# A Mamba-2 layer with a gated LoRA branch: B times C and the sum of squares as column halves right behind the mixing, and x's transposes ahead of the state's product

## What is computed

```
proj = xn @ in_proj_w.T                       # gate 4096, x 4096, B 1024, C 1024, dt 64
xBC  = silu(conv_bias + sum_k pad(hbc)[k:] * conv_weight[:, k])      # 4 taps
dt_p = softplus(dt + dt_bias);  dA = exp(dt_p * A)
state = state * dA_t + (dt_p * x)_t * B_t;    y_t = state . C_t      # for every token
y  = y + x * D
yn = y * rsqrt(mean(y * y over the 512 channels of a group) + EPS) * norm_weight * silu(gate)
out = yn @ out_proj_w.T
```

## Time and profile before

| | |
|---|---|
| three runs, us | 1832.69, 1836.27, 2473.83 |
| median, us | 1836.27 |
| profiled execution, us | 1833.52 |
| its span, first to last instruction, us | 1831.7 |
| mean granted TensorE clock | 0.994 |
| busy: TensorE, weight loads | 1791.5 (98%), 1425.5 (78%) |
| busy: VectorE, ScalarE, GpSimd | 1526.6 (83%), 812.5 (44%), 1170.5 (64%) |
| HBM | 119 GB/s over the span |

### The profile page before, as it was taken

The page is one execution under the profiler, slowest core; times in us unless marked ns, Lnnn a source line. Parts: engine busy times, 40 slices in busy tenths (PEclk is TensorE's granted clock), DMA queues, the critical chain, the costliest instruction groups (busy, mean ns, idle before and its releaser), DMA issues.

```text
span 1831.7 us, 29420 instructions
## 1 busy us (share of the span) xinstructions
PE 1791.5 (98%) x10904; PEld 1425.5 (78%) x10904; DVE 1526.6 (83%) x1945; ACT 812.5 (44%) x1803; POOL 1170.5 (64%) x1149
## 2 busy tenths in 40 slices
PE   6989999999999999999999999999999999999997
PEld 4777877878787787878777787777878778787875
DVE  6868888888888888888888888888888888888887
ACT  4554353444435344443544434354444435444442
POOL 5437557574755757475697847658574765857478
PEclk9999999999999999999999999999999999999998
DMA  7542224232333423333564333323232323323233
GB/s 244 162 132 104 104 104 138 84 125 104 104 105 103 138 89 120 104 105 108 181 228 140 125 104 123 104 102 129 76 128 102 122 104 104 132 75 117 91 126 130
DMA packets 113502, 220.70 MB, mean 120 GB/s; under 512 B 10448, under 2 KB 46672, under 8 KB 113360
## 3 DMA queue, kind: packets, MB, share of 16 engines
q1 hardware_dynamic: 112320, 218.66, 35.7%
q10 hardware_dynamic: 1040, 0.16, 0.1%
HBM read 204.63 MB, written 14.16 MB: 119 GB/s over the span
## 4 chain that ended last, share of the span: by engine, by line
PE 87%; DVE 4%; POOL 3%; ACT 2%; issue 2%; DMA 1%; SPq 0%; POOLq 0%; DVEq 0%; ACTq 0%
PE ps_conv L1148 9%; PE ps_conv L1151 9%; PE ps_conv L1154 7%; PE ps_y L1308 6%; PE ps_out L1151 6%; PE ps_out L1148 6%; PE ps_gate L1148 6%; PE ps_gate L1151 6%; PE ps_y L1313 5%; PE ps_s L1336 5%; PE ps_out L1154 5%; PE ps_gate L1154 4%; PE turned_x L1234 3%; PE ps_conv L1155 2%; PE ps_g L1273 2%
## 5 line engine op out<-in xcount | busy, mean ns | idle before, releaser
L801 DVE SCALAR_TENSOR_TENSOR xc<-ps_conv,convw_sb,xc 128x511 f32<-128x511 f32 (+2 forms) x576 | 429.8, 746 | 26.2 <-ACT xc L589 12.0
L1083 POOL TENSOR_TENSOR rstd_col<-mean_square,half 128x1 f32<-128x1 f32 x128 | 105.5, 825 | 541.2 <-ACT mean_square L719 541.2
L974 DVE TENSOR_TENSOR decay<-decay,ps_g 128x1024 f32<-128x1024 f32 x128 | 155.9, 1218 | 175.6 <-PE ps_g L1346 175.6
L910 DVE TENSOR_TENSOR_SCAN decay<-decay,eye 128x1024 f32<-128x1024 f32 x128 | 297.6, 2325 | 0.6 <-DMA decay<-decays_d 0.6
L595 ACT ACTIVATE xc<-xc 128x512 f32<-128x512 f32 x192 | 120.9, 631 | 381.6 <-DVE xc L801 380.8
L1101 POOL TENSOR_TENSOR cpre<-cpre,xc 128x1024 f32<-128x1024 f32 x112 | 267.5, 2388 | 0.0
L1148 PE MATMUL ps_conv<-xn_hi,wconv_hi 128*128 128x512 f32 x768 | 242.4, 437 | 0.0
L1151 PE MATMUL ps_conv<-xn_hi,wconv_lo 128*128 128x512 f32 x768 | 207.1, 392 | 0.0
L1308 PE MATMUL ps_y<-decay,dtx 128*64 128x128 f32 x2048 | 197.4, 279 | 2.1 <-DVE decay L974 1.9
L728 ACT ACTIVATE square<-ps_y 128x512 f32<-128x512 f32 x128 | 76.7, 599 | 244.0 <-DVE ps_y L925 244.0
L1148 PEld LDWEIGHTS ps_conv<-xn_hi,wconv_hi 128*128 128x128 f32 x768 | 140.1, 193 | 49.1 <-issue 29.9
(11 more groups left out here) (206 smaller groups left out, 3734.3 us busy)
## 6 DMA issues: line engine op xcount, KB each, us to landing
decay<-decays_d SPq DMA_DIRECT2D x128, 512.0 KB, 5.3
cpre<-rows_d SPq DMA_DIRECT2D x112, 512.0 KB, 3.9
stage<-w_in_t SPq DMA_DIRECT2D x32, 1024.0 KB, 6.5
stage<-w_out_t SPq DMA_DIRECT2D x16, 1024.0 KB, 5.3
stage<-w_in_t SPq DMA_DIRECT2D x32, 256.0 KB, 3.3
out_sum<-hidden SPq DMA_DIRECT2D x16, 256.0 KB, 6.1
ffn_d<-sgate SPq DMA_DIRECT2D x16, 256.0 KB, 2.4
out<-out_sum SPq DMA_DIRECT2D x16, 256.0 KB, 3.8
```

What stands on the lines that cost most here:

```text
L801: e.scalar_tensor_tensor(acc[:, d:], ps[:, 0:BLK - d], convw_sb[:, tile, TAPS - 1 - d:TAPS - d], acc[:, d:], ALU.mult, ALU.add).then_inc(S ...
L910: e.tensor_tensor_scan(d[:, :], d[:, :], eye8[:, :, :].rearrange("p h i -> p (h i)"), 0.0, ALU.mult, ALU.add).then_inc(S["scan"], 1)
L974: e.tensor_tensor(by_head(d[:, :]), by_head(d[:, :]), ps_g[:, P:2 * P].unsqueeze(1).to_broadcast([P, GH, P]), ALU.mult).then_inc(S["M"], 1)
```

## The change

B times C is no longer the last thing of an iteration. It stands right behind the mixing, ahead of the sum of squares, and it is made of two `matmul`s of 64 columns, the first into partitions 0 to 63 of the bank and the second into 64 to 127 (`halves`). The sum of squares is made in the same way. The transposes of the next chunk's x move from behind the late convolution to a place behind the gate's projection. The wait for ScalarE's two reads of the bank moves from B times C on TensorE to the multiplication by it on VectorE. The numbers of values computed stay the same.

```diff
@@ -970,6 +970,9 @@
                 if i < N:
                     w.wait_ge(S["scan"], i + 1)
                     w.wait_ge(S["mm_g"], i + 1)
+                    w.wait_ge(S["var2"], u + 1 if u >= 0 else 0)
+                    if i % NCH < NCH - 1:
+                        w.wait_ge(S["b_tok"], inner(i))
                     w.wait_ge(S["last"], inner(i))
                     e.tensor_tensor(by_head(d[:, :]), by_head(d[:, :]),
                                     ps_g[:, P:2 * P].unsqueeze(1).to_broadcast([P, GH, P]),
@@ -1140,6 +1143,11 @@
         def _(e):
             w = Waits(e)
 
+            def halves(ps, a, b):
+
+                e.matmul(ps[0:HD, :], a[:, 0:HD], b, start=True, stop=True, skip_group_check=True)
+                return e.matmul(ps[HD:, :], a[:, HD:], b, start=True, stop=True, skip_group_check=True)
+
             def passes(ps, a, b, n, second, third, done):
 
 
@@ -1270,8 +1278,7 @@
                 w.wait_ge(S["eye"], 3)
                 w.wait_ge(S["sum2"], u + 1)
                 w.wait_ge(S["M"], min(u + DRAIN, N))
-                e.matmul(ps_g[:, 2 * P:2 * P + 1], square_sum[:, :], ones[:, :], start=True, stop=True,
-                         skip_group_check=True).then_inc(S["mm_ssq"], 1)
+                halves(ps_g[:, 2 * P:2 * P + 1], square_sum[:, :], ones[:, :]).then_inc(S["mm_ssq"], 1)
 
             def yn_lo_ready(u):
 
@@ -1313,6 +1320,13 @@
                                 mixed = e.matmul(y_h, before[:, h * HD:(h + 1) * HD], c_left[:, h, :], start=False,
                                                  stop=True, skip_group_check=True)
                     mixed.then_inc(S["mm_in"], 1)
+                if i < N:
+                    w.wait_ge(S["silu"], max(conv_no(i // CPB, t) for t in (XT, XT + 1)) + 1)
+                    w.wait_ge(S["var2"], u if u >= 0 else 0)
+                    w.wait_ge(S["b_tok"], inner(m) if m >= 0 else 0)
+                    w.wait_ge(S["M"], i)
+                    w.wait_ge(S["lo"], TOK)
+                    halves(ps_g[:, P:2 * P], xb[:, XT, cc], xb[:, XT + 1, cc]).then_inc(S["mm_g"], 1)
                 if 0 <= u < N - 1:
                     sum_squares(u)
                 if i < N and i % NCH < NCH - 1:
@@ -1325,6 +1339,8 @@
                     conv(conv_early(i))
                 for k in gated(i):
                     gate(k)
+                if i + 1 < N:
+                    turn_xc(i + 1)
                 late_first = i < N and conv_early(i) is None and conv_late(i) is not None
                 if late_first:
                     conv(conv_late(i))
@@ -1336,15 +1352,6 @@
                     e.matmul(ps_s[:, :], b_tok[:, :], xw[:, :], start=True, stop=True).then_inc(S["mm_u"], 1)
                 if i < N and conv_late(i) is not None and not late_first:
                     conv(conv_late(i))
-                if i + 1 < N:
-                    turn_xc(i + 1)
-                if i < N:
-                    w.wait_ge(S["silu"], conv_no(i // CPB, XT + 1) + 1)
-                    w.wait_ge(S["var2"], u + 1 if u >= 0 else 0)
-                    if i % NCH < NCH - 1:
-                        w.wait_ge(S["b_tok"], inner(i))
-                    e.matmul(ps_g[:, P:2 * P], xb[:, XT, cc], xb[:, XT + 1, cc], start=True, stop=True,
-                             skip_group_check=True).then_inc(S["mm_g"], 1)
 
 
 def kernel(L0_attn_hidden_states, L0_attn_in_proj_w, L0_attn_conv_weight, L0_attn_conv_bias, L0_attn_dt_bias,
```

## The result

The changed kernel took 1818.25 us (median of six runs, 1816.63 to 1818.86) against 1834.48 us for the kernel before (median of six, five of them between 1832.22 and 1836.5, the sixth, 2473.83, far from them; without it the median is 1832.69, and the later experiments have 1832.65 to 1833.35 for the same kernel): a ratio of 0.991, 95% interval 0.990 to 0.992. The profiled execution spans 1817.0 us against 1831.7, that is 14.7 us less, at a granted clock of 0.993 against 0.994. The forecast was 1810 us in a range from 1801 to 1831, a gain of 23.8 us. The time fell into the range, and by over 2% neither faster nor slower. The gain is 14.4 to 16.2 us, by the one median or the other: six to seven tenths of what was forecast.

The account below looks back on a forecast made before the run. The prediction took the intervals between TensorE's starts to bound the steady part and VectorE the end. From 1833.5 us it took 20.3 for the halved sum of squares and 3.5 for the end: 1810 us, range 1801 to 1831.

Parts of the forecast that it names:

- What bounds the kernel: Steady part: TensorE bounds the kernel, and the time is the sum of intervals between its instruction starts.
- B times C, moved and split: Behind the mixing, two 64-column halves take 0.22 us, against 0.21 to 0.22 at the iteration's end: zero.
- The sum of squares in halves: From the mixing's end to the next projection's second pass: 0.16 us less, 127 times, 20.3 us.
- The rival by which one column costs a mixing step: TensorE's one-column halves go at 0.11 us a pair, no steady gain: 1830 us; chance 0.13.
- x's transposes at no cost: Moved behind the gate's projection, they take 0.44 us wherever they stand among 128-column work: zero by themselves.
- the check of xw's time: In iteration 36 xw is done 1.03 us before the gate ends, so the moved transposes cost no wait.
- no TensorE wait at the moved transposes: Sign expected in the profile after: TensorE doesn't wait at x's transposes in their new place.
- VectorE and the end: Last iterations: VectorE's waits for B times C go, 2.6 us, plus 0.9 elsewhere: 3.5 us, between 0 and 6.
- VectorE is the bound: At the end, where no projection fills TensorE, VectorE was taken as the bound.
- The sum: Whole kernel: 20.3 us from the halves plus 3.5 at the end, 23.8 us gained, forecast 1810 us.

Follow-up runs that it names:

- experiment 1: The changed kernel with the sum of squares whole again, one 128-column matmul in the same place: 1834.08 us, ratio 1.0006 to the kernel before.
- experiment 2: The kernel before with only the sum of squares in halves and nothing moved: 1816.34 us, ratio 0.9913.
- experiment 3: The changed kernel with x's transposes back behind the late convolution: 1816.07 us, ratio 0.9906 to the kernel before.
- experiment 4: The changed kernel with B's transpose between B times C and the sum of squares, cutting the 64-column run in two: 1849.76 us, ratio 1.0090.
- experiment 5: The changed kernel with the two halves of the sum of squares computed twice: 1828.94 us, ratio 0.9976 to the kernel before.
- experiment 8: GpSimd's last addition cut from 512 to 4 columns in the last five iterations: 1813.89 us in the changed kernel, 1831.19 us in the kernel before.
- experiment 9: The kernel of experiment 3 with the last four iterations' skip (x times D) moved from GpSimd to ScalarE: 1813.52 us, ratio 0.9894.
- experiment 7: The changed kernel with GpSimd's skip (x times D) ahead of its squares in the last three iterations: 1817.07 us, ratio 0.9913.

## Why the prediction was right, and what it mis-sized

**What bounds the kernel** was right for the steady part: what the distances between TensorE's starts lost in the intervals is what the time lost.

**B times C, moved and split, costs nothing:** right. It takes the forecast 0.22 us, and experiments 1 to 3 show that its move and its halves give some 0.02 us an iteration or nothing.

**The sum of squares in halves:** right, mechanism and size. The two stretches measure 0.27 and 0.33 to 0.34 as forecast, the change of form 0.10 and a pair of small loads 0.05 to 0.06 where the earlier trace rows gave 0.05 (experiments 4 and 5). Experiment 3 has the term nearly by itself: 18.6 us in 112 intervals, 0.166 on average and 0.178 outside the uneven nine, where 0.16 was forecast; experiment 2, which has the halves alone, gives 0.155 outside them. The rival by which one column costs a mixing step fell. Of the rule on overhead in the Trainium skill, TensorEngine Tiling (Array Packing), section Instruction Overhead, by which one column lasts as long as 60 and no tiling factor is to be taken from a small dimension, the trace shows why it doesn't forbid the halves here: before, one instruction held TensorE for 0.12 us, and its halves are 0.03 to 0.06 apart, so it was held by its 128-column load, which the halves shorten, and not by its one streamed column.

**x's transposes at no cost:** the step that failed in size. The sentence "wherever they stand among 128-column work: zero by themselves" took the 0.44 us from one place. Where a block begins, between two projections, they cost 0.06 more than between the state's product and the output projection; in the other iterations the move costs nothing by itself, as forecast. And the check of xw's time looked at the transposes' own wait only, not at what they had covered: with 0.66 us less between the late convolution and the mixing, VectorE's multiplication ends last in each group's fourth chunk. The two together are 3.2 us, the sums of intervals of experiment 3 and of the changed kernel (18.6 less 15.4). The forecast "no TensorE wait at the moved transposes" held in the steady part but for one wait of 0.5 us, not at the two ends of the program.

**VectorE and the end:** the term of 3.5 us, forecast between 0 and 6, was wrong in sign, -2.7. The two waits for B times C did go. TensorE's wait at the state's product in the last iterations shrank from 5.4 to 1.7, but 2.5 turned up at the transposes ahead of it and 0.6 at the output projections. And the step "VectorE is the bound" was read from the group of waits that is longest, while GpSimd, which has no idle row from the first to the last of its four power rows, goes at the same pace of 10.6 us in both kernels. The lead of the changed kernel tells where the term went: 17.3 us at mixing 123, 16.9 at GpSimd's first power row, 16.8 at its last and at the output projection that follows TensorE's long stop, 14.7 at the end. What VectorE won turned into a wait for GpSimd, and that into one long stop of TensorE: no gain, 0.6 us lost. The other 2.1 are lost behind that stop, 1.9 of them to the clock. Its last two output projections in the changed kernel with the mixing between them, and the first of them and that mixing in the kernel before:

```profile
1798.24 2.08 PE L1156 MATMUL ps_out<-wout_hi,ynt_hi 128*128 128x512 f32 x4 [4.88 <-DVE out_sum L960]
...
1803.15 0.44 PE L1315 MATMUL ps_y<-decay,dtx 128*64 128x128 f32 x4
...
1808.00 1.17 PE L1156 MATMUL ps_out<-wout_hi,ynt_hi 128*128 128x512 f32 x4 [2.83 <-DVE out_sum L960]
```

```profile
1815.01 1.20 PE L1148 MATMUL ps_out<-wout_hi,ynt_hi 128*128 128x512 f32 x4 [2.06 <-DVE out_sum L960]
...
1818.01 0.44 PE L1308 MATMUL ps_y<-decay,dtx 128*64 128x128 f32 x4
```

After 4.88 us without work the granted clock is 0.50 from 1797 to 1802 us, the lower of the two levels, and four products take 2.08 us instead of 1.20; in the kernel before it is 1.00 from 1813 to 1818. There it had been low under two state's products instead (1.84 and 2.04 us for 1.10, at 1793.15 and 1803.76), in iterations that GpSimd paces, so that it cost nothing. From the projection's start to the mixing are 4.91 us (1798.24 to 1803.15) against 3.00 (1815.01 to 1818.01): 1.9 of the 2.7 us. Experiments 8 and 9, in which GpSimd is relieved, take back 4.2 and 2.1 us of the stretch from mixing 123 on. So the failed step is the path: GpSimd, not VectorE alone, sets the pace of the end. How much of the loss behind it belongs to the change is open: every other kernel of the experiments takes 19.4 to 20.3 us behind the last power row against 18.1 in the kernel before, also the one of experiment 8 that has nothing of the change, and there is one profile of each. What decides in which product the low clock falls wasn't taken further.

**The sum** with measured sizes: 18.6 for the halves in 112 intervals and 0.4 in the next three, less 3.2 for the transposes and 2.7 at the end, is 13.1; with 1.6 of the start, which can't be put down to the change (from 0.9 lost to 2.6 gained in the other kernels), 14.7, the difference of the spans.

## What to carry to other kernels

Where a matmul streams next to nothing, look at its weight load: here that was its price, 0.24 us, and halves brought it down by 0.16. Put the narrow products into one run of the same tile form: a run cut in two cost 0.34 us more. After a stop of TensorE look at the granted clock of what follows it, and whether that product is on the path. A step that is moved at no cost of its own may have been the cover of somebody else: ask what it stood behind, and what became due earlier when it left. Before a saving on the longest waiter is counted, look at every engine for stretches without an idle row; where two have one, both must be relieved.

## What the hardware showed unexpectedly

At the end of both kernels, a short GpSimd instruction that meets VectorE's scan lasts until the scan has ended. The changed kernel, GpSimd's sum of squares beside the scan and one iteration later without it:

```profile
1789.74 2.28 DVE L910 TENSOR_TENSOR_SCAN decay<-decay,eye 128x1024 f32<-128x1024 f32 x1
1789.78 2.50 POOL L1113 TENSOR_TENSOR square_sum<-square 128x128 f32<-128x128 f32 x1
...
1800.45 0.46 POOL L1113 TENSOR_TENSOR square_sum<-square 128x128 f32<-128x128 f32 x1
```

0.46 us became 2.50, up to 1792.28, the scan ending at 1792.02; the instruction behind it starts at 1792.24, so the time is real. The same happened to a skip (3.02 for 1.04) and to the outputs' multiplication (3.26 for 1.27), 2.0 us more each time, once in each round of the end. Moving the skip ahead (experiment 7) moved the collision to the squares: 2.32 us for 0.46 in one round and 2.72 for 0.74 in the next.

The Trainium skill, SBUF — State Buffer, section Who interferes with whom, says that VectorE and GpSimd share a pair of ports under an exclusive lock, and that a VectorE instruction with two inputs in SBUF contends for it with a GpSimd instruction that reads SBUF. The scan has two such inputs, and all these GpSimd instructions read SBUF; the trace agrees. The page doesn't name the scan.
